# The phase features of the first self-attention: folding, squares and products move from GpSimd and VectorE, and the division by the root mean square comes last

## The chip, the core and the metric

One core of a Trainium2 chip runs the whole program, a transformer of four layers with 14 stages of its own kind. The core has TensorE (PE), VectorE (DVE), ScalarE (ACT), GpSimd (POOL) and SyncE (SP), each with its own queue of instructions; they wait for each other on semaphores. The metric is the time of one execution on the device in microseconds, as the median of several; lower is better.

## What is computed

The change lies in layer 0's self-attention. With 1024 tokens (32 sequences of 32), 256 channels in 16 heads of 16, it builds, besides the usual query and key, a sine and a cosine feature of each, scaled by a normalized amplitude:

```python
def _amp_norm(t):
    a = jax.nn.softplus(t)
    return a / jnp.sqrt(jnp.mean(a * a, axis=-1, keepdims=True) + AMP_EPS)
...
q_amp = _amp_norm(q)
k_amp = _amp_norm(k)
q_phi = math.pi * jnp.tanh(split(x @ Wqp))
k_phi = math.pi * jnp.tanh(split(x @ Wkp))
q_cos = q_amp * jnp.cos(q_phi)
q_sin = q_amp * jnp.sin(q_phi)
k_cos = k_amp * jnp.cos(k_phi)
k_sin = k_amp * jnp.sin(k_phi)
scores_phase = (einsum(q_cos, k_cos) + einsum(q_sin, k_sin)) * scale
lam = (LAMBDA_MAX * jnp.tanh(lambda_raw))[None, :, None, None]
scores = scores_dot + lam * scores_phase
```

## The kernel before

The program is a list of stages. Each stage is one block: every engine gets its own straight list of instructions, the order is the order in which the code is written, and a barrier of all engines ends the stage. `phase_features` is such a stage. `prepare` (projections) runs ahead of it and leaves queries and keys in `qk` and the raw phases in `ph`, both 128 partitions x 2 halves x 2048 numbers: half u=0 is of the queries, u=1 of the keys, channels lie on partitions and tokens along the row. `self_attention` follows, and takes `qk`, `sn` and `cs`.

In the stage, softplus(t) is built as max(t, 0) + ln(1 + exp(-|t|)) with a correction for the rounding of 1 + exp. VectorE makes the magnitudes (line 1625), ScalarE the exp (1668), VectorE "plus" and "rest" (1628, 1631), ScalarE the Ln (1672), VectorE the sum, the amplitude and its square (1635, 1638, 1640). TensorE sums the squares of each head of 16 channels, with tokens on partitions (1709: for each half 16 products with a 0/1 matrix of 8 columns, into PSUM bank 4 or 5). ScalarE takes the root (1682), VectorE the reciprocal (1645), ScalarE spreads each value over its 16 channels (1687), and TensorE transposes the result back, four transposes for a PSUM bank of 512 columns, eight banks in all (1717). VectorE multiplies the amplitude by each bank (1650).

Beside this, ScalarE takes tanh of the phases (1665), then the sine (1676) and, as sin(pi/2 - pi |x|), the cosine (1679). The magnitude |x| for it is made by GpSimd as 2 max(x, 0) - x, in `cs` (1695 and 1697). Last come the products of sine and cosine with the normalized amplitude: those of the queries with half of tanh(lambda) as well, on VectorE (1656, for each of the two rows of 1024), the cosine of the keys on VectorE (1658), the sine of the keys on GpSimd (1700).

The functions `stage`, `buffers` and `spread` are helpers; `k.ps` is PSUM with 8 banks.

Of the kernel before, what the change touches and what calls it, by code (L numbers as in the profile page):

```python
# [18 lines left out]
ALU = mybir.AluOpType  # L19
ACT = mybir.ActivationFunctionType  # L20
# [8 lines left out]
DC = D // P  # L29
# [183 lines left out]
@contextmanager  # L213
def stage(k, names):

    k.stages += 1
    sems = {n: k.nc.alloc_semaphore(name=f"{n}_{k.stages}") for n in names.split()}
    clear_retired(k)
    with k.nc.Block() as block:
        yield block, namedtuple("Semaphores", sems)(**sems)  # L220
    k.retired = list(sems.values())
# [9 lines left out]
@contextmanager  # L231
def buffers(k, dtype=F32, **shapes):

    with ExitStack() as ctx:
        k.buffers += 1
        made = {n: ctx.enter_context(k.nc.sbuf_tensor(f"{n}_{k.buffers}", list(s), dtype)) for n, s in shapes.items()}
        yield namedtuple("Buffers", made)(**made)
# [51 lines left out]
def spread(ap, n, axis):  # L289

    shape = list(ap.shape)
    return ap.unsqueeze(axis).broadcast_to(shape[:axis] + [n] + shape[axis:])
# [1316 lines left out]
def phase_features(k, w, qk, ph, amp, sn, cs):  # L1609


    nc = k.nc
    PI = float(np.float32(np.pi))
    names = ("abs_done exp_done plus_done rest_done ln_done sum_done amp_done square_done sums_done root_done recip_done spread_done wide_done "
             "norm_done tanh_done rise_done fold_done sin_done cos_done lam_tanh lam_done const_done")
    with stage(k, names) as (block, s), \
            buffers(k, f=[P, 2, DC, T], rms=[P, 2, 2, NT, DC, 8], eps=[P, 1], half=[P, 1], lam=[P, 2, DC]) as b:
        def roots(u):

            return b.f[:, u].rearrange("p c t -> p (c t)").rearrange("p (a ch) -> p a ch", ch=P)  # L1620

        @block.vector
        def _(dve):
            for u in range(2):
                nc.vector.scalar_tensor_tensor(amp[:, u], qk[:, u], -1.0, qk[:, u], ALU.mult, ALU.max).then_inc(s.abs_done, 1)
            for u in range(2):
                dve.wait_ge(s.exp_done, u + 1)
                nc.vector.tensor_scalar(b.f[:, u], amp[:, u], 1.0, None, ALU.add).then_inc(s.plus_done, 1)
                dve.wait_ge(s.plus_done, u + 1)

                nc.vector.scalar_tensor_tensor(amp[:, u], b.f[:, u], -1.0, amp[:, u], ALU.add,
                                               ALU.subtract).then_inc(s.rest_done, 1)
            for u in range(2):
                dve.wait_ge(s.ln_done, u + 1)
                nc.vector.scalar_tensor_tensor(b.f[:, u], qk[:, u], 0.0, b.f[:, u], ALU.max, ALU.add).then_inc(s.sum_done, 1)
                dve.wait_ge(s.sum_done, u + 1)
                dve.wait_ge(s.rest_done, u + 1)
                nc.vector.tensor_tensor(amp[:, u], b.f[:, u], amp[:, u], ALU.subtract).then_inc(s.amp_done, 1)
                dve.wait_ge(s.amp_done, u + 1)
                nc.vector.tensor_tensor(b.f[:, u], amp[:, u], amp[:, u], ALU.mult).then_inc(s.square_done, 1)  # L1640
            dve.wait_ge(s.lam_tanh, 1)
            nc.vector.tensor_scalar(b.lam[:, 1], b.lam[:, 0], 0.5, None, ALU.mult).then_inc(s.lam_done, 1)
            for u in range(2):
                dve.wait_ge(s.root_done, u + 1)
                nc.vector.reciprocal(b.rms[:, 1, u], b.rms[:, 0, u]).then_inc(s.recip_done, 1)
            for u in range(2):
                for q in range(4):
                    dve.wait_ge(s.wide_done, 4 * u + q + 1)
                    part = amp[:, u, q // 2, (q % 2) * 512:(q % 2) * 512 + 512]
                    nc.vector.tensor_tensor(part, part, k.ps[:, 4 * u + q, :], ALU.mult).then_inc(s.norm_done, 1)  # L1650
            dve.wait_ge(s.norm_done, 8)
            dve.wait_ge(s.lam_done, 1)
            for done, t in ((s.sin_done, sn), (s.cos_done, cs)):
                dve.wait_ge(done, 2)
                for c in range(DC):
                    nc.vector.scalar_tensor_tensor(t[:, 0, c], t[:, 0, c], b.lam[:, 1, c:c + 1], amp[:, 0, c],
                                                   ALU.mult, ALU.mult)
            nc.vector.tensor_tensor(cs[:, 1], cs[:, 1], amp[:, 1], ALU.mult)

        @block.scalar  # L1660
        def _(act):
            act.wait_ge(*w.at)
            nc.scalar.activation(b.lam[:, 0], w.lam, ACT.Tanh).then_inc(s.lam_tanh, 1)
            for u in range(2):
                nc.scalar.activation(ph[:, u], ph[:, u], ACT.Tanh).then_inc(s.tanh_done, 1)
            for u in range(2):
                act.wait_ge(s.abs_done, u + 1)
                nc.scalar.activation(amp[:, u], amp[:, u], ACT.Exp, scale=-1.0).then_inc(s.exp_done, 1)
            for u in range(2):
                act.wait_ge(s.plus_done, u + 1)  # L1670
                act.wait_ge(s.rest_done, u + 1)
                nc.scalar.activation(b.f[:, u], b.f[:, u], ACT.Ln).then_inc(s.ln_done, 1)
            act.wait_ge(s.tanh_done, 2)
            act.wait_ge(s.const_done, 2)
            for u in range(2):
                nc.scalar.activation(sn[:, u], ph[:, u], ACT.Sin, scale=PI).then_inc(s.sin_done, 1)
            for u in range(2):
                act.wait_ge(s.fold_done, u + 1)
                nc.scalar.activation(cs[:, u], cs[:, u], ACT.Sin, bias=b.half[:, 0:1], scale=-PI).then_inc(s.cos_done, 1)
            for u in range(2):  # L1680
                act.wait_ge(s.sums_done, u + 1)
                nc.scalar.activation(b.rms[:, 0, u].rearrange("p t c h -> p (t c h)"), k.ps[:, 4 + u, 0:P], ACT.Sqrt,
                                     bias=b.eps[:, 0:1], scale=1.0 / 16).then_inc(s.root_done, 1)
            for u in range(2):
                act.wait_ge(s.recip_done, u + 1)
                inverse = b.rms[:, 1, u].rearrange("p t c h -> p (t c h)")
                nc.scalar.copy(roots(u).rearrange("p a (h d) -> p (a h) d", d=16), spread(inverse, 16, 2)).then_inc(s.spread_done, 1)

        @block.gpsimd
        def _(pool):  # L1690
            nc.gpsimd.memset(b.eps[:], 1e-6).then_inc(s.const_done, 1)
            nc.gpsimd.memset(b.half[:], PI / 2).then_inc(s.const_done, 1)
            for u in range(2):
                pool.wait_ge(s.tanh_done, u + 1)
                nc.gpsimd.tensor_scalar(cs[:, u], ph[:, u], 0.0, 2.0, ALU.max, ALU.mult).then_inc(s.rise_done, 1)
                pool.wait_ge(s.rise_done, u + 1)
                nc.gpsimd.tensor_tensor(cs[:, u], cs[:, u], ph[:, u], ALU.subtract).then_inc(s.fold_done, 1)
            pool.wait_ge(s.norm_done, 8)
            pool.wait_ge(s.sin_done, 2)
            nc.gpsimd.tensor_tensor(sn[:, 1], sn[:, 1], amp[:, 1], ALU.mult)  # L1700

        @block.tensor
        def _(pe):
            for u in range(2):
                pe.wait_ge(s.square_done, u + 1)
                for t in range(NT):
                    for c in range(DC):
                        at = (t * DC + c) * 8
                        mm = nc.tensor.matmul(k.ps[:, 4 + u, at:at + 8], b.f[:, u, c, t * P:(t + 1) * P], k.head8,
                                              start=True, stop=True)  # L1710
                mm.then_inc(s.sums_done, 1)
            for u in range(2):
                pe.wait_ge(s.spread_done, u + 1)
                for c in range(DC):
                    for half in range(2):
                        for t in range(4):
                            mm = nc.tensor.transpose(k.ps[:, 4 * u + 2 * c + half, t * P:(t + 1) * P],
                                                     roots(u)[:, (half * 4 + t) * DC + c, :], k.ident)
                        mm.then_inc(s.wide_done, 1)
# [1091 lines left out]
```

## Time and profile before

| | us |
|---|---|
| median of 3 executions | 2239.22 (2233.44 to 2244.39) |
| the profiled execution | 2251.26, its span 2249.4 |
| granted TensorE clock in it, mean share of full speed | 0.829 |
| VectorE busy in the span | 1016.7 (45%) |
| ScalarE busy | 733.2 (33%) |
| GpSimd busy | 484.8 (22%) |
| TensorE matmuls busy | 1676.2 (75%) |

The shares are means over all stages. The stage of this change stands around 269 to 344 us of the span. A timeline row shows when a run of equal instructions starts, how long it lasts in all, and in brackets for how long the engine stood idle before and on whom it waited.

### The profile page before, as it was taken

Reading aid. Unit: us, or ns where it says so; the run is one execution under the profiler, and the core shown is the slowest. Engines: PE = TensorE matmul, PEld = TensorE weight load, DVE = VectorE, ACT = ScalarE, POOL = GpSimd, SP = SyncE. Lnnn points to the kernel's source line nnn. Section 1 sums busy time; section 2 is a strip of 40 time slices with the busy share of each in tenths; the row PEclk is TensorE's granted clock in tenths of the full one; section 3 lists DMA queues with packets and bytes.
Section 4 is the critical chain, followed back from the end, with each engine's and each line's share of the span. In section 5 each row is a group of like instructions: output and inputs, shape, how many; then the busy total and the mean of one; then the engine's idle time right before and its main releaser. Section 6 shows DMA issues by size and latency. Waiting matters only on the chain. (4 is left out here: it accounts for less than half of the span.)

```text
span 2249.4 us, 54254 instructions
## 1 busy us (share of the span) xinstructions
PE 1676.2 (75%) x22206; PEld 1443.7 (64%) x22206; DVE 1016.7 (45%) x2187; ACT 733.2 (33%) x1631; POOL 484.8 (22%) x643
## 2 busy tenths in 40 slices
PE   5998635769966888674888479976488967767684
PEld 4886535569965777563777368863377945655583
DVE  5565483321126777326111446544755733334313
ACT  3554331114433455220233145431223322322121
POOL 3442242002223333100344222210002200010141
PEclk9999755569988999765999689997687988666697
DMA  3220000049962110003899511100100162000485
GB/s 136 55 50 18 3 0 3 27 159 343 342 239 69 45 41 26 5 4 103 265 309 298 175 30 44 47 27 0 40 23 29 38 215 72 4 2 9 144 282 179
DMA packets 84817, 219.27 MB, mean 97 GB/s; under 512 B 19720, under 2 KB 38472, under 8 KB 77072
## 3 DMA queue, kind: packets, MB, share of 16 engines
q1 hardware_dynamic: 76464, 194.14, 26.2%
q0 software_dynamic: 8160, 22.29, 3.1%
q8 instruction: 153, 2.51, 0.5%
q14 instruction: 40, 0.33, 0.0%
HBM read 200.92 MB, written 15.34 MB: 96 GB/s over the span
## 5 line engine op out<-in xcount | busy, mean ns | idle before, releaser
L2227 ACT ACTIVATE g<-ps,b 128x128 f32<-128x128 f32 x340 | 125.0, 368 | 288.7 <-PE ps L2189 267.4
L2189 PEld LDWEIGHTS ps<-xt,w 128*128 128x128 f32 x1728 | 212.6, 197 | 8.7 <-issue 4.2
L2189 PE MATMUL ps<-xt,w 128*128 128x128 f32 x1728 | 213.5, 280 | 2.7 <-DVE xt L2368 2.1
L2199 PE MATMUL ps<-w,g 128*128 128x256 f32 x864 | 206.6, 387 | 0.0
L2199 PEld LDWEIGHTS ps<-w,g 128*128 128x128 f32 x864 | 161.2, 195 | 19.4
L2245 POOL DMA_INDIRECT x<-rows,token x85 | 83.3, 980 | 316.7 <-DVEq L2344 283.0
L484 PE MATMUL ps<-x,w 128*128 128x512 f32 x408 | 119.9, 460 | 34.8 <-DVE x L581 34.8
L2250 POOL DMA_INDIRECT results<-y,dest x85 | 83.7, 985 | 284.2 <-DVE y L2381 225.6
L2368 DVE COPY xt<-ps 128x256 f32<-128x256 f32 x85 | 36.1, 425 | 235.6 <-PE ps L2179 235.6
L484 PEld LDWEIGHTS ps<-x,w 128*128 128x128 f32 x408 | 91.9, 229 | 61.1 <-DVE x L581 39.9
L468 PE MATMUL ps<-consts_sb,z_sb 128*128 128x128 f32 x176 | 34.9, 365 | 112.1 <-DVE z_sb L567 112.0
L468 PEld LDWEIGHTS ps<-consts_sb,z_sb 128*128 128x128 f32 x176 | 28.4, 188 | 119.3 <-DVE z_sb L567 117.8
L733 PE MATMUL ps<-c,w 128*128 128x258 f32 x512 | 97.7, 304 | 8.5 <-DVE pt L1031 4.6
L733 PEld LDWEIGHTS ps<-c,w 128*128 128x128 f32 x512 | 78.3, 198 | 21.9 <-issue 11.5
L743 PE MATMUL ps<-w,c 128*128 128x256 f32 x512 | 91.5, 291 | 0.0
L769 PE MATMUL ps<-consts_sb,p 128*128 128x128 f32 x512 | 68.8, 277 | 28.6 <-ACT key L859 28.5
L2381 DVE TENSOR_TENSOR y<-ps,b 128x256 f32<-128x256 f32 x62 | 26.3, 425 | 132.7 <-PE ps L2199 132.7
L1913 PE MATMUL ps<-x,w 128*128 128x512 f32 x288 | 80.0, 419 | 7.7 <-DVE w L2052 7.7
L869 ACT ACTIVATE p<-sc,nmax 128x257 f32<-128x257 f32 x128 | 58.3, 503 | 82.3 <-DVE nmax L996 82.3
L2179 PE MATMUL ps<-consts_sb,x 128*128 128x128 f32 x170 | 35.9, 295 | 61.8 <-DMA x<-rows,token 61.6
L984 DVE TENSOR_TENSOR val<-ps,store_sb 128x512 f32<-128x512 f32 x64 | 44.2, 691 | 83.3 <-PE ps L743 82.9
L1926 PEld LDWEIGHTS ps<-w,g 128*128 128x128 f32 x576 | 76.3, 194 | 7.8 <-issue 3.6
(410 smaller groups left out, 3744.3 us busy)
## 6 DMA issues: line engine op xcount, KB each, us to landing
w<-in_L_ffn_w SPq DMA_DIRECT2D x124, 512.0 KB, 4.9
w<-in_L_ffn_w SPq DMA_DIRECT2D x46, 1024.0 KB, 7.5
c<-in_ctx SPq DMA_DIRECT2D x96, 258.0 KB, 2.7
b<-in_w_L_ffn SPq DMA_DIRECT2D x62, 128.0 KB, 6.7
rows<-in_w_L_xattn SPq DMA_DIRECT2D x8, 768.0 KB
c<-in_w_L_xattn SPq DMA_DIRECT2D x8, 514.0 KB
back<-results SPq DMA_DIRECT2D x16, 256.0 KB, 4.5
raw<-in_L_ffn_w SPq DMA_DIRECT2D x16, 256.0 KB, 3.5
```

The source lines that it names most:

```text
L468: mm = nc.tensor.transpose(k.ps[:, 2 * half + c, t * P:(t + 1) * P], z[:, half * HT + t, c * P:(c + 1) * P], k.ident)
L484: mm = nc.tensor.matmul(bank, r.w[:, p1, c, col:col + P], r.x[:, p2, c, half * 512:(half + 1) * 512], start=i == 0 and c == 0, stop=i == 2 ...
L733: last = nc.tensor.matmul(k.ps[:, KB + c, 0:LP], wp, cp, start=t == 0, stop=t == 4)
L743: last = nc.tensor.matmul(k.ps[:, VB, half * D:(half + 1) * D], cp, wp, start=t == 0, stop=t == 4)
L769: last = nc.tensor.transpose(k.ps[:, TB + pair, at:at + P], b.p[:, par, r4, half * P:(half + 1) * P], k.ident)
L1913: mm = nc.tensor.matmul(k.ps[:, slot(j, h), :], r.w1[:, j // 2, p1, c, h * P:(h + 1) * P], r.x[:, p2, c, (j % 2) * 512:(j % 2 + 1) * 512], ...
L1926: mm = nc.tensor.matmul(k.ps[:, 4 + t, 0:D], r.g[:, p1, slot(j, h), t * P:(t + 1) * P], r.w2[:, j // 2, p2, h, :], start=h == 0 and i == 0 ...
L2189: mm = nc.tensor.matmul(hidden_bank(par, h), b.w1[:, par, c, h * P:(h + 1) * P], b.xt[:, par, c, :], start=c == 0, stop=c == DC - 1)
L2199: mm = nc.tensor.matmul(k.ps[:, YB + par, 0:D], b.g[:, par, h, :], b.w2[:, par, h, :], start=h == 0, stop=h == HC - 1)
L2227: nc.scalar.activation(b.g[:, par, h, :], hidden_bank(par, h), func, bias=b.b1[:, par, h:h + 1]).then_inc(s.g_ready, 1)
L2245: nc.gpsimd.indirect_dma_start(b.x[:, n % 2, :], None, k.rows, bass.IndirectOffsetOnAxis(ap=u.token[:, n:n + 1], axis=0)).then_inc(x_loade ...
L2250: nc.gpsimd.indirect_dma_start(k.results, bass.IndirectOffsetOnAxis(ap=u.dest[:, n:n + 1], axis=0), b.y[:, n % 2, :], None).then_inc(sent[ ...
```

## The change

GpSimd has no block in the stage any more. Its three kinds of work go elsewhere: the two constants are set by VectorE, |x| is one ScalarE activation (Abs) for each half, and the sine of the keys is multiplied on VectorE. The squares go from VectorE to ScalarE (Square), the first between the sines and the cosines, the second behind the cosines. The second tanh goes behind the exps.

The order of the last products is turned round. Before, the amplitude was divided by its root mean square (eight products with PSUM banks) and then multiplied into sine and cosine. Now sine and cosine are multiplied by the raw amplitude (and lambda) first, and then each of them by the PSUM banks: sixteen products. TensorE waits for both roots before it writes the transposes, as it did before through the order of the work.

```diff
         @block.vector
         def _(dve):
+            nc.vector.memset(b.eps[:], 1e-6).then_inc(s.const_done, 1)
+            nc.vector.memset(b.half[:], PI / 2).then_inc(s.const_done, 1)
...
-                dve.wait_ge(s.amp_done, u + 1)
-                nc.vector.tensor_tensor(b.f[:, u], amp[:, u], amp[:, u], ALU.mult).then_inc(s.square_done, 1)
...
+            dve.wait_ge(s.amp_done, 2)
+            dve.wait_ge(s.lam_done, 1)
+            for done, t in ((s.sin_done, sn), (s.cos_done, cs)):
+                dve.wait_ge(done, 1)
+                for c in range(DC):
+                    nc.vector.scalar_tensor_tensor(t[:, 0, c], t[:, 0, c], b.lam[:, 1, c:c + 1], amp[:, 0, c],
+                                                   ALU.mult, ALU.mult).then_inc(s.scaled, 1)
+                dve.wait_ge(done, 2)
+                nc.vector.tensor_tensor(t[:, 1], t[:, 1], amp[:, 1], ALU.mult).then_inc(s.scaled, 1)
...
+            dve.wait_ge(s.scaled, 6)
             for u in range(2):
                 for q in range(4):
                     dve.wait_ge(s.wide_done, 4 * u + q + 1)
-                    part = amp[:, u, q // 2, (q % 2) * 512:(q % 2) * 512 + 512]
-                    nc.vector.tensor_tensor(part, part, k.ps[:, 4 * u + q, :], ALU.mult).then_inc(s.norm_done, 1)
...
+                    for t in (sn, cs):
+                        part = t[:, u, q // 2, (q % 2) * 512:(q % 2) * 512 + 512]
+                        nc.vector.tensor_tensor(part, part, k.ps[:, 4 * u + q, :], ALU.mult)
...
         @block.scalar
         def _(act):
...
+            nc.scalar.activation(ph[:, 1], ph[:, 1], ACT.Tanh).then_inc(s.tanh_done, 1)
+            for u in range(2):
+                act.wait_ge(s.tanh_done, u + 1)
+                nc.scalar.activation(cs[:, u], ph[:, u], ACT.Abs).then_inc(s.fold_done, 1)
...
+            act.wait_ge(s.amp_done, 1)
+            nc.scalar.activation(b.f[:, 0], amp[:, 0], ACT.Square).then_inc(s.square_done, 1)
...
+            act.wait_ge(s.amp_done, 2)
+            nc.scalar.activation(b.f[:, 1], amp[:, 1], ACT.Square).then_inc(s.square_done, 1)
...
-        @block.gpsimd
-        def _(pool):
...
-                nc.gpsimd.tensor_scalar(cs[:, u], ph[:, u], 0.0, 2.0, ALU.max, ALU.mult).then_inc(s.rise_done, 1)
-                pool.wait_ge(s.rise_done, u + 1)
-                nc.gpsimd.tensor_tensor(cs[:, u], cs[:, u], ph[:, u], ALU.subtract).then_inc(s.fold_done, 1)
-            pool.wait_ge(s.norm_done, 8)
-            pool.wait_ge(s.sin_done, 2)
-            nc.gpsimd.tensor_tensor(sn[:, 1], sn[:, 1], amp[:, 1], ALU.mult)
...
         def _(pe):
...
+            pe.wait_ge(s.root_done, 2)
```

The compiled order of ScalarE's instructions in the stage, the kernel before against the changed one; `ACT_TABLE_LOAD` brings in the tables of the functions that follow:

```order
-L1663 ACT_TABLE_LOAD
-L1663 ACTIVATE lam<-store_sb 128x2
-L1665 ACTIVATE ph<-ph 128x2048 x2
-L1668 ACTIVATE amp<-amp 128x2048 x2
-L1672 ACT_TABLE_LOAD
-L1672 ACTIVATE f<-f 128x2048 x2
-L1676 ACT_TABLE_LOAD
-L1676 ACTIVATE sn<-ph 128x2048 x2
-L1679 ACTIVATE cs<-cs,half 128x2048 x2
-L1682 ACT_TABLE_LOAD
-L1682 ACTIVATE rms<-ps,eps 128x128 x2
-L1687 COPY f<-rms 128x2048 x2
```

```order
+L1671 ACT_TABLE_LOAD
+L1671 ACTIVATE lam<-store_sb 128x2
+L1672 ACTIVATE ph<-ph 128x2048
+L1675 ACTIVATE amp<-amp 128x2048 x2
+L1676 ACTIVATE ph<-ph 128x2048
+L1679 ACTIVATE cs<-ph 128x2048 x2
+L1683 ACT_TABLE_LOAD
+L1683 ACTIVATE f<-f 128x2048 x2
+L1686 ACT_TABLE_LOAD
+L1686 ACTIVATE sn<-ph 128x2048 x2
+L1688 ACTIVATE f<-amp 128x2048
+L1691 ACTIVATE cs<-cs,half 128x2048 x2
```

Four activations of 128x2048 are added (1679 twice, 1688, and 1693 behind the cosines), the second tanh stands behind the exps, and the number of table loads is the same: the fourth one, for the root, stands behind 1693.

VectorE's part from the amplitudes on, of the kernel before and then of the changed one, first half of the banks:

```order
-L1638 TENSOR_TENSOR amp<-f,amp 128x2048
-L1640 TENSOR_TENSOR f<-amp 128x2048
-L1642 TENSOR_SCALAR lam<-lam 128x2
-L1645 RECIPROCAL rms<-rms 128x128 x2
-L1650 TENSOR_TENSOR amp<-amp,ps 128x512 x8
-L1656 SCALAR_TENSOR_TENSOR sn<-sn,lam,amp 128x1024 x2
-L1656 SCALAR_TENSOR_TENSOR cs<-cs,lam,amp 128x1024 x2
-L1658 TENSOR_TENSOR cs<-cs,amp 128x2048
```

```order
+L1636 TENSOR_TENSOR amp<-f,amp 128x2048
+L1653 SCALAR_TENSOR_TENSOR sn<-sn,lam,amp 128x1024 x2
+L1656 TENSOR_TENSOR sn<-sn,amp 128x2048
+L1653 SCALAR_TENSOR_TENSOR cs<-cs,lam,amp 128x1024 x2
+L1656 TENSOR_TENSOR cs<-cs,amp 128x2048
+L1659 RECIPROCAL rms<-rms 128x128 x2
+L1666 TENSOR_TENSOR sn<-sn,ps 128x512
+L1666 TENSOR_TENSOR cs<-cs,ps 128x512
```

The products with sine and cosine have moved from behind the reciprocals and banks to ahead of them, and the bank products are pairs, eight pairs in all.

## Rows read from the trace of the kernel before

**Rows 1.** The page's first line: the span and the instructions

```profile
span 2249.4 us, 54254 instructions
```

**Rows 2.** Busy time by stretch: stretch, length, each engine, granted clock, DMA share, GB/s

```profile
262.00:346.00 84.00, 25.15 (x134) 24.10 (x132) 66.96 (x35) 31.35 (x26) 34.08 (x10) 0.59 0.00 0
```

**Rows 3.** VectorE's timeline of the stage: start us, duration us, instruction, idle before

```profile
275.90 5.64 DVE L1628 TENSOR_SCALAR f<-amp 128x2048 f32<-128x2048 f32 x1 [2.39 <-ACT amp L1668]
281.58 6.46 DVE L1631 SCALAR_TENSOR_TENSOR amp<-f,amp 128x2048 f32<-128x2048 f32 x1
287.96 8.09 DVE L1628 TENSOR_SCALAR f<-amp 128x2048 f32<-128x2048 f32 x1
296.09 6.46 DVE L1631 SCALAR_TENSOR_TENSOR amp<-f,amp 128x2048 f32<-128x2048 f32 x1
302.47 2.28 DVE L1635 SCALAR_TENSOR_TENSOR f<-qk,f 128x2048 f32<-128x2048 f32 x1
...
307.11 2.29 DVE L1640 TENSOR_TENSOR f<-amp 128x2048 f32<-128x2048 f32 x1
...
323.74 0.95 DVE L1645 RECIPROCAL rms<-rms 128x128 f32<-128x128 f32 x1 [5.90 <-ACT rms L1682]
326.70 0.69 DVE L1650 TENSOR_TENSOR amp<-amp,ps 128x512 f32<-128x512 f32 x1 [2.01 <-PE ps L1717]
...
328.41 3.85 DVE L1650 TENSOR_TENSOR amp<-amp,ps 128x512 f32<-128x512 f32 x6 [0.17 <-PE ps L1717]
332.30 6.81 DVE L1656 SCALAR_TENSOR_TENSOR sn<-sn,lam,amp 128x1024 f32<-128x1024 f32 x2
339.04 2.47 DVE L1656 SCALAR_TENSOR_TENSOR cs<-cs,lam,amp 128x1024 f32<-128x1024 f32 x2
341.43 2.28 DVE L1658 TENSOR_TENSOR cs<-cs,amp 128x2048 f32<-128x2048 f32 x1
```

**Rows 4.** ScalarE's timeline of the stage

```profile
268.97 1.28 ACT L1663 ACT_TABLE_LOAD   x1 [1.82 <-PEq L219]
...
270.38 3.69 ACT L1665 ACTIVATE ph<-ph 128x2048 f32<-128x2048 f32 x2
...
302.64 1.91 ACT L1672 ACTIVATE f<-f 128x2048 f32<-128x2048 f32 x1 [11.32 <-DVE amp L1631]
...
305.86 3.71 ACT L1676 ACTIVATE sn<-ph 128x2048 f32<-128x2048 f32 x2
309.48 3.88 ACT L1679 ACTIVATE cs<-cs,half 128x2048 f32<-128x2048 f32 x2
```

**Rows 5.** GpSimd's timeline of the stage

```profile
272.36 8.10 POOL L1695 TENSOR_SCALAR cs<-ph 128x2048 f32<-128x2048 f32 x1 [2.98 <-ACT ph L1665]
280.55 5.34 POOL L1697 TENSOR_TENSOR cs<-cs,ph 128x2048 f32<-128x2048 f32 x1
285.86 9.11 POOL L1695 TENSOR_SCALAR cs<-ph 128x2048 f32<-128x2048 f32 x1
295.06 5.34 POOL L1697 TENSOR_TENSOR cs<-cs,ph 128x2048 f32<-128x2048 f32 x1
332.34 4.49 POOL L1700 TENSOR_TENSOR sn<-sn,amp 128x2048 f32<-128x2048 f32 x1 [31.94 <-DVE amp L1650]
```

**Rows 6.** Groups of instructions by form, VectorE: busy us, mean ns, idle before

```profile
L554 DVE MEMSET eps<- 128x1 f32 x14 | 0.8, 59 | 4.7 <-PEq L219 4.7
```

**Rows 7.** TensorE's timeline of the stage

```profile
309.46 13.85 PE L1709 MATMUL ps<-consts_sb,f 128*128 128x8 f32 x64 [41.50 <-DVE f L1640]
325.55 5.34 PE L1717 MATMUL ps<-consts_sb,f 128*128 128x128 f32 x32 [2.24 <-ACT f L1687]
```

**Rows 8.** Busy time by stretch of 50 us, columns as in rows 2

```profile
350.00:400.00 50.00, 35.93 (x1428) 30.32 (x1427) 12.90 (x29) 9.80 (x20) 9.12 (x10) 0.53 0.02 4
...
500.00:550.00 50.00, 50.00 (x346) 47.11 (x346) 5.94 (x14) 20.02 (x55) 13.08 (x14) 1.00 0.95 337
```

More of the change, by code:

```diff
@@ L1614, in phase_features @@
     names = ("abs_done exp_done plus_done rest_done ln_done sum_done amp_done square_done sums_done root_done recip_done spread_done wide_done "
-             "norm_done tanh_done rise_done fold_done sin_done cos_done lam_tanh lam_done const_done")
+             "tanh_done fold_done sin_done cos_done lam_tanh lam_done const_done scaled")
     with stage(k, names) as (block, s), \
@@ L1623, in _, with plus @@
         def _(dve):
-            for u in range(2):
-                nc.vector.scalar_tensor_tensor(amp[:, u], qk[:, u], -1.0, qk[:, u], ALU.mult, ALU.max).then_inc(s.abs_done, 1)
-            for u in range(2):
+            def plus(u):
                 dve.wait_ge(s.exp_done, u + 1)
@@ L1632, in _, with amplitude @@
                                                ALU.subtract).then_inc(s.rest_done, 1)
-            for u in range(2):
+            def amplitude(u):
                 dve.wait_ge(s.ln_done, u + 1)
@@ L1638, in _ @@
                 nc.vector.tensor_tensor(amp[:, u], b.f[:, u], amp[:, u], ALU.subtract).then_inc(s.amp_done, 1)
-                dve.wait_ge(s.amp_done, u + 1)
-                nc.vector.tensor_tensor(b.f[:, u], amp[:, u], amp[:, u], ALU.mult).then_inc(s.square_done, 1)
+            nc.vector.memset(b.eps[:], 1e-6).then_inc(s.const_done, 1)
+            nc.vector.memset(b.half[:], PI / 2).then_inc(s.const_done, 1)
+            for u in range(2):
+                nc.vector.scalar_tensor_tensor(amp[:, u], qk[:, u], -1.0, qk[:, u], ALU.mult, ALU.max).then_inc(s.abs_done, 1)
+            for u in range(2):
+                plus(u)
             dve.wait_ge(s.lam_tanh, 1)
@@ L1643, in _ @@
             for u in range(2):
+                amplitude(u)
+            dve.wait_ge(s.amp_done, 2)
[7 more added lines that the diff above has]
+                nc.vector.tensor_tensor(t[:, 1], t[:, 1], amp[:, 1], ALU.mult).then_inc(s.scaled, 1)
+            for u in range(2):
                 dve.wait_ge(s.root_done, u + 1)
                 nc.vector.reciprocal(b.rms[:, 1, u], b.rms[:, 0, u]).then_inc(s.recip_done, 1)
+            dve.wait_ge(s.scaled, 6)
             for u in range(2):
@@ L1648, in _ @@
                     dve.wait_ge(s.wide_done, 4 * u + q + 1)
-                    part = amp[:, u, q // 2, (q % 2) * 512:(q % 2) * 512 + 512]
-                    nc.vector.tensor_tensor(part, part, k.ps[:, 4 * u + q, :], ALU.mult).then_inc(s.norm_done, 1)
[L1651 to L1658, printed above, removed]
+                    for t in (sn, cs):
+                        part = t[:, u, q // 2, (q % 2) * 512:(q % 2) * 512 + 512]
+                        nc.vector.tensor_tensor(part, part, k.ps[:, 4 * u + q, :], ALU.mult)
         @block.scalar
@@ L1663, in _ @@
             nc.scalar.activation(b.lam[:, 0], w.lam, ACT.Tanh).then_inc(s.lam_tanh, 1)
-            for u in range(2):
-                nc.scalar.activation(ph[:, u], ph[:, u], ACT.Tanh).then_inc(s.tanh_done, 1)
+            nc.scalar.activation(ph[:, 0], ph[:, 0], ACT.Tanh).then_inc(s.tanh_done, 1)
             for u in range(2):
@@ L1668, in _ @@
                 nc.scalar.activation(amp[:, u], amp[:, u], ACT.Exp, scale=-1.0).then_inc(s.exp_done, 1)
+            nc.scalar.activation(ph[:, 1], ph[:, 1], ACT.Tanh).then_inc(s.tanh_done, 1)
+            for u in range(2):
+                act.wait_ge(s.tanh_done, u + 1)
+                nc.scalar.activation(cs[:, u], ph[:, u], ACT.Abs).then_inc(s.fold_done, 1)
             for u in range(2):
@@ L1672, in _ @@
                 nc.scalar.activation(b.f[:, u], b.f[:, u], ACT.Ln).then_inc(s.ln_done, 1)
-            act.wait_ge(s.tanh_done, 2)
             act.wait_ge(s.const_done, 2)
@@ L1687, in _ @@
                 nc.scalar.copy(roots(u).rearrange("p a (h d) -> p (a h) d", d=16), spread(inverse, 16, 2)).then_inc(s.spread_done, 1)
-        @block.gpsimd
-        def _(pool):
[L1691 to L1694, printed above, removed]
-                nc.gpsimd.tensor_scalar(cs[:, u], ph[:, u], 0.0, 2.0, ALU.max, ALU.mult).then_inc(s.rise_done, 1)
-                pool.wait_ge(s.rise_done, u + 1)
-                nc.gpsimd.tensor_tensor(cs[:, u], cs[:, u], ph[:, u], ALU.subtract).then_inc(s.fold_done, 1)
-            pool.wait_ge(s.norm_done, 8)
-            pool.wait_ge(s.sin_done, 2)
-            nc.gpsimd.tensor_tensor(sn[:, 1], sn[:, 1], amp[:, 1], ALU.mult)
         @block.tensor
```

## The prediction

> **What bounds the kernel now.** The program is a chain of stages with a barrier between each two, so I asked where in the span of 2249.4 us [rows 1] the changed stage stands and what ends last in it. The view of busy time by stretch, cut at the stage's edges (262 to 346 us), shows that no engine is at its limit there: VectorE (DVE) is busy 67 of 84 us, TensorE 25, ScalarE (ACT) 31, GpSimd (POOL) 34, and the DMA engines move nothing [rows 2]. The stage is a chain of dependent steps, and no transfer runs under it that could become the limit once it is shorter. It starts with a table load on ACT at 268.97 and ends with VectorE's last product at 341.43 + 2.28 = 343.71, so it is 74.7 us long [rows 3, 4].
>
> Read VectorE's timeline first [rows 3]. Lines 1635 and 1640 take 2.28 and 2.29 us for 128x2048 with two SBUF inputs. Line 1631 is the same kind and shape as line 1635, yet it takes 6.46. Line 1628 takes 5.64 and then 8.09. Line 1656 is four equal instructions: the sn pair takes 6.81 us, the cs pair 2.47. Now lay GpSimd's timeline beside it [rows 5]. GpSimd's instructions end at 280.46, 285.89, 294.97 and 300.40. VectorE's end at 281.54, 288.04, 296.05 and 302.55: 1.08, 2.15, 1.08 and 2.15 us later. At the stage's end GpSimd finishes its product at 336.83, while the first sn instruction of line 1656 is still open. Each of these VectorE instructions is long as if it stood still until GpSimd's was done, and then ran in its own time. I read this as: while GpSimd works in SBUF, these VectorE instructions do not move. So 275.90 to 302.55, 26.65 us, is GpSimd's time on VectorE's account, and ACT stands waiting for it (11.32 us ahead of the second Ln alone [rows 4]).
>
> The Trainium skill says so too ("Advanced Engine Details and Errata", the notes on VectorE's two SBUF ports): the second one is shared with GpSimd, and the instructions of the one block those of the other. Its "VectorE: DVE Perf Modes" (the perf-mode tier table) gives 1227 ns for a lone fp32 tensor_scalar of 2048; with the trace's 1.08 or with this figure the sum below is the same.
>
> **The change, step by step**, on the clock of the trace. I rebuild the stage with durations of rows, and put its end against 343.71.
>
> ACT becomes the first bound. From 270.38 it runs six 128x2048 instructions in a row (tanh, exp, exp, tanh, abs, abs). Pairs of such take 3.69 us, 1.845 each [rows 4]: 11.1 us, to 281.5. What they wait for is there: VectorE's first magnitude is done at about 269.1 + 2.3 = 271.4 and the second at 273.6 (the two memsets that it now runs first are 0.06 each [rows 6]); the first exp can start at 272.2. Abs is nowhere in the trace. Every other function of this shape takes 3.69 to 3.88 a pair [rows 4], so its bounds are 1.84 and 1.94 each; I take 1.845, and two of them and two Squares can be 0.4 us off. The compiled order shows four table loads in the stage before and after.
>
> VectorE under it: plus and rest for each half. The first exp ends at 274.1. Line 1628 alone is at least the remainder of 1.08 and at most the 2.29 of a two-input product; rest is 2.28. So both halves are done between 280.9 and 283.3, and the second is needed at 284.7. Either end is hidden behind ACT. That is where VectorE's stall goes.
>
> ACT goes on: table load 1.28 (as in [rows 4]) to 282.8; Ln and Ln, the first ends at 284.7, the second at 286.5; table load to 287.8; two Sin, 3.71, to 291.5; Square of half 0, 1.85, to 293.35; two cosines, 3.88, to 297.2; Square of half 1, to 299.1. VectorE's amplitudes come at 284.7 + 2 x 2.28 = 289.3 and 293.9, both before their Squares. So half 0's Square is late by the sine ahead of it, about 2 us.
>
> TensorE: the sums of squares are 64 matmuls of line 1709 in 13.85 us [rows 7], 6.93 a half and back to back. They now run from 293.4 to 300.3 and on to 307.25; the second Square is done long before 300.3. Before, they ended at 323.31. This is the gain of the first part: **16.1 us**.
>
> From the last sum to VectorE's first product with a PSUM bank the way is the same: root, reciprocal, spread copy on ACT, four transposes. It was 326.70 - 323.31 = 3.39 us [rows 3, 7]. The new wait (TensorE for both roots) is met before the spread copy, and holds only the transposes. In the shadow of the sums, VectorE now does the scaling by lambda and amplitude: sn 2.47 + 2.28, cs the same, from 293.9 to 303.4. The first half's reciprocal (0.95 us [rows 3]) lands at 304.4, with room to 307.6, where ACT's spread copy first asks for it; were the scaling longer than that, the excess would go straight to the end. So the first bank product starts at 307.25 + 3.4 = 310.65.
>
> The tail: before, 8 bank products to 332.3, then 11.4 us to 343.71 (with GpSimd's product in it, 4.49 us that held VectorE's). Now 16 bank products. Six at full pace took 3.85 us [rows 3], 0.63 from start to start and 0.69 for the last: 15 x 0.632 + 0.69 = 10.2 us. Transposes come at 0.86 us a bank ((328.41 - 326.70) / 2), and each bank now feeds 1.26 us of VectorE, so TensorE isn't late. The end is at 310.65 + 10.2 = **320.8**. Before, it was 17.0 us from the first bank product to the end; now 10.2: **6.8 us**.
>
> Sum: 16.1 + 6.8 = 22.9 us. The following stage waits for the barrier only, nothing is loaded under this one for it, and GpSimd, with no work here now, waits at the barrier as it waits today; so it starts 22.9 us earlier.
>
> One rule of the Trainium skill speaks against the edit ("ScalarE: Activation LUTs", rules for kernel authors): additions and products belong on VectorE. The trace has 1.85 us on ACT against 2.29 on VectorE for 128x2048 fp32. By the rule the Squares would stay on VectorE, right behind each amplitude, and the sums would start at 291.6 and not at 293.4; the stage would then be 1.8 us shorter still, so the rule costs this change a little and does not turn it.
>
> **Rivals.**
> *A: the long VectorE instructions are long by themselves* (in-place, or that operation), not held by GpSimd. For it: both of line 1631 take exactly 6.46. Against it: line 1656, the same pair at 6.81 and at 2.47 within 9 us, and the ends that follow GpSimd's. Worked out: 26.65 us from 274.1 end at 300.8; the second Ln at 302.7; table load and sines to 307.7; Squares at 309.6 and 315.3; sums to 323.5; 3.4 and 10.2 more: 337.0. The gain is 6.7 us, 2232.5.
>
> *B: TensorE's clock helps.* The attention that follows runs at a mean granted 0.53 of full speed (350 to 400 us), close to the 1.2 GHz level [rows 8]. It would start 8 us after the last transpose, not 15.9 before. If more of it is granted 2.4 GHz, some of its 36 us of matmuls in each 50 are shorter: 10 us more, about 2206. Other phases of those lifts, without a trend, are worth 3 us to either side.
>
> *C: slower.* The expert loop that follows is at 50.00 of 50 us of TensorE at a granted 1.00, in three such stretches from 500 to 650 [rows 8]. If the shifted start makes the clock stay at 1.2 GHz there, 150 us of full-speed work is worth up to 150 us more. It decides from the point where 23 us of it fall to the lower level; for 2250 it takes 34. Nothing shows the clock to fall under such a load, and the loop's own entry is not changed. 3 in 100.
>
> *D: the change doesn't do what it says*: GpSimd's seven instructions of the stage are gone in the compiled order, so that is excluded; what is left is Abs and Square at twice the price on ACT; three of them (both Abs and the first Square), 5.6 us, are on the path: 2221.9. 3 in 100, inside the range.
>
> **The numbers.** The profiled execution was 2251.26 us, 12 above the median of 2239.22; the difference of two stage lengths carries over unchanged: 2239.2 - 22.9 = 2216.3. Forecast 80 in 100 (with D), A 8, B 8, C 3, something unseen 1. The forecast's own range is 3 us of clock phase, 2 of durations, and the 5 us by which single executions stand off the median: 2208 to 2225. For 8 in 10 I take in part of A and all of B: 2206 to 2229. A measurement of this kernel can tell 0.5%, 11.2 us, from no change, so "faster" is below 2228: the forecast and B give 0.88. Same, 0.09, is A and a forecast that misses by half; slower 0.03.
>
> **What would show it.** VectorE's lines for plus and rest at about 1.1 and 2.3 us (if 6, A holds). ACT without a wait until the second Square. First sum at 24.4 us after the stage's first table load, first bank product at 41.7, end at 51.8. Sixteen bank products 0.63 apart. If the stage is 52 us long and the total hasn't fallen by 23, look at the granted clock between 320 and 500 us.

## The result, and the profile after

The changed kernel took 2212.51 us (median of 4; 2207.03 to 2220.06), beside 2240.95 us for the kernel before in the same measurement: ratio 0.988, 95% interval 0.9841 to 0.9919. Two further series of it gave 0.9899 (0.9867 to 0.9931) and 0.989 (0.9861 to 0.9918). The change makes the kernel faster, by some 25 us: 0.989 of 2240 is 24.6 us off. The profiled execution has a span of 2218.2 us.

The stage itself went from 74.74 us to 51.20 (from its first table load to the end of VectorE's last product, 268.39 to 319.59), 23.5 us less. First ScalarE's timeline in the changed kernel: start us, duration us, instruction, and in brackets the idle time before it with its cause. It answers to [rows 4].

```profile
268.39 1.28 ACT L1671 ACT_TABLE_LOAD   x1 [1.82 <-PEq L219]
...
277.00 3.69 ACT L1679 ACTIVATE cs<-ph 128x2048 f32<-128x2048 f32 x2
280.71 1.28 ACT L1683 ACT_TABLE_LOAD   x1
282.00 3.71 ACT L1683 ACTIVATE f<-f 128x2048 f32<-128x2048 f32 x2
...
287.03 3.71 ACT L1686 ACTIVATE sn<-ph 128x2048 f32<-128x2048 f32 x2
290.64 1.89 ACT L1688 ACTIVATE f<-amp 128x2048 f32<-128x2048 f32 x1
...
306.45 0.37 ACT L1696 ACTIVATE rms<-ps,eps 128x128 f32<-128x128 f32 x1 [6.46 <-PE ps L1710]
```

From 269.69 to 298.14 no row has a wait; the 11.32 us of [rows 4] are gone. Abs (line 1679) takes 3.69 us a pair, as every other function does, and Square (1688) 1.89 alone.

VectorE's timeline, against [rows 3]; lines 1626 and 1628 are the plus and rest that were 1628 and 1631:

```profile
273.52 1.23 DVE L1626 TENSOR_SCALAR f<-amp 128x2048 f32<-128x2048 f32 x1 [0.53 <-ACT amp L1675]
274.79 2.29 DVE L1628 SCALAR_TENSOR_TENSOR amp<-f,amp 128x2048 f32<-128x2048 f32 x1
276.99 1.22 DVE L1626 TENSOR_SCALAR f<-amp 128x2048 f32<-128x2048 f32 x1
278.25 2.29 DVE L1628 SCALAR_TENSOR_TENSOR amp<-f,amp 128x2048 f32<-128x2048 f32 x1
...
302.32 0.94 DVE L1659 RECIPROCAL rms<-rms 128x128 f32<-128x128 f32 x1
306.84 0.95 DVE L1659 RECIPROCAL rms<-rms 128x128 f32<-128x128 f32 x1 [3.58 <-ACT rms L1696]
309.94 0.69 DVE L1666 TENSOR_TENSOR sn<-sn,ps 128x512 f32<-128x512 f32 x1 [2.14 <-PE ps L1719]
310.54 0.68 DVE L1666 TENSOR_TENSOR cs<-cs,ps 128x512 f32<-128x512 f32 x1
...
318.91 0.68 DVE L1666 TENSOR_TENSOR cs<-cs,ps 128x512 f32<-128x512 f32 x1
```

The same four instructions that took 5.64, 6.46, 8.09 and 6.46 us with GpSimd at work beside them take 1.23, 2.29, 1.22 and 2.29. The scaling and the first reciprocal are over at 303.26, well before the second root, and VectorE then waits 3.58 us for it. The sixteen bank products run without a gap, 0.60 us from start to start. TensorE's timeline, against [rows 7]:

```profile
292.59 13.82 PE L1710 MATMUL ps<-consts_sb,f 128*128 128x8 f32 x64 [25.20 <-ACT f L1688]
308.74 5.80 PE L1719 MATMUL ps<-consts_sb,f 128*128 128x128 f32 x32 [2.33 <-ACT f L1701]
```

| from the stage's first table load, us | before | forecast | after |
|---|---|---|---|
| start of the first sum of squares | 40.5 | 24.4 | 24.2 |
| end of the last sum of squares | 54.3 | 38.3 | 38.0 |
| start of the first bank product | 57.7 | 41.7 | 41.6 |
| end of the stage | 74.7 | 51.8 | 51.2 |

### The profile page after: what moved, and what is told of

The parts are those of the page before. It is cut to its first block and busy times, and to the rows that moved or that the text cites. A ratio compares the mean times of both kernels' runs of the same rounds, so it can differ in the third digit from the quotient of the medians.

```text
span 2218.2 us, 54260 instructions
## 1 busy us (share of the span) xinstructions
PE 1674.4 (75%) x22206; PEld 1440.5 (65%) x22206; DVE 993.9 (45%) x2196; ACT 737.2 (33%) x1635; POOL 452.2 (20%) x636
## 5 line engine op out<-in xcount | busy, mean ns | idle before, releaser
L2201 PE MATMUL ps<-w,g 128*128 128x256 f32 x864 | 202.8, 382 | 0.0
L1928 PE MATMUL ps<-w,g 128*128 128x256 f32 x576 | 77.7, 286 | 3.5 <-DVE g L2028 3.5
```

The costliest lines, as they stand in the source:

```text
L1928: mm = nc.tensor.matmul(k.ps[:, 4 + t, 0:D], r.g[:, p1, slot(j, h), t * P:(t + 1) * P], r.w2[:, j // 2, p2, h, :], start=h == 0 and i == 0 ...
L2201: mm = nc.tensor.matmul(k.ps[:, YB + par, 0:D], b.g[:, par, h, :], b.w2[:, par, h, :], start=h == 0, stop=h == HC - 1)
```

## The experiments

The theory: 18 us of the gain are VectorE's freedom from GpSimd's folding; the rest is the turned order of the products and GpSimd's last product. The rival: the long VectorE instructions were long by the old order or by themselves. All stage lengths below are measured as above. Most of them repeat closely: 51.20 us in all three traces of the changed kernel, 45.31 and 45.32 in two of the reordered one, and 74.74 and 74.56 in two of the kernel before. One kernel, the first below, has 57.65 and 56.62. The totals do not repeat so well, which has its own paragraph below.

**One part alone: Abs on ScalarE in the kernel before.**

```diff
+            for u in range(2):
+                act.wait_ge(s.tanh_done, u + 1)
+                nc.scalar.activation(cs[:, u], ph[:, u], ACT.Abs).then_inc(s.fold_done, 1)
...
-                nc.gpsimd.tensor_scalar(cs[:, u], ph[:, u], 0.0, 2.0, ALU.max, ALU.mult).then_inc(s.rise_done, 1)
-                pool.wait_ge(s.rise_done, u + 1)
-                nc.gpsimd.tensor_tensor(cs[:, u], cs[:, u], ph[:, u], ALU.subtract).then_inc(s.fold_done, 1)
```

> The kernel before with one part of the change alone: |x| for the cosine is ScalarE's Abs, GpSimd does no folding. Squares, the order of the products and GpSimd's last product stay. If GpSimd's folding held VectorE, plus and rest take 1.2 and 2.3 us and not 5.6 to 8.1, the sums of squares end about 36.2 us after the stage's first table load (before 54.3), and the stage is 56.6 us long (before 74.7): 18 us less, about 2222. If plus and rest are long by themselves, they stay at 26.6 us together and the stage loses at most 5 us.

Plus and rest took 1.23, 2.29, 1.22 and 2.29 us, the sums of squares ended 36.4 us into the stage, and the stage was 57.65 us long, 17.1 less than before. Its tail still had GpSimd's last product. VectorE's timeline of this kernel near the stage's end, and under it GpSimd's:

```profile
319.31 6.82 DVE L1656 SCALAR_TENSOR_TENSOR sn<-sn,lam,amp 128x1024 f32<-128x1024 f32 x2
326.05 2.47 DVE L1656 SCALAR_TENSOR_TENSOR cs<-cs,lam,amp 128x1024 f32<-128x1024 f32 x2
...
319.35 4.49 POOL L1698 TENSOR_TENSOR sn<-sn,amp 128x2048 f32<-128x2048 f32 x1 [45.87 <-DVE amp L1650]
```

Two equal pairs of VectorE, 6.82 beside GpSimd and 2.47 without: 4.35 us of waiting for a product that costs VectorE 2.28 if it does it itself. The total however was only 10.5 us lower (ratio 0.9951, 0.9933 to 0.9968), which left 6 us unexplained, so it ran again:

> The kernel before with ScalarE's Abs for the folding, again. Its stage was 17.1 us shorter, but its total only 10.5 (7 to 15). If the missing 6 us are scatter of the other stages, this run gives 17 within 4 us. If GpSimd's absence costs something later, it gives 10 again.

It gave 0.9922 (0.9896 to 0.9948), 17.5 us, with a stage of 56.62 us. Here the stage's gain is carried over in full. The first interval alone did not contain 17, and why that total gained less is not shown; the paragraph on scatter comes back to it. The two stages differ by 1.03 us at the transposes: TensorE took 6.67 us for them at a granted clock of 0.54 in the first trace, and 5.03 us at 0.73 in the second. In the first, VectorE waited for a transpose before six more of its eight banks, which then start 0.85 us apart; in the second before two, and the others start 0.60 apart.

**The folding given back to GpSimd, in the changed kernel.**

```diff
-                nc.scalar.activation(cs[:, u], ph[:, u], ACT.Abs).then_inc(s.fold_done, 1)
...
+                nc.gpsimd.tensor_scalar(cs[:, u], ph[:, u], 0.0, 2.0, ALU.max, ALU.mult).then_inc(s.rise_done, 1)
+                pool.wait_ge(s.rise_done, u + 1)
+                nc.gpsimd.tensor_tensor(cs[:, u], cs[:, u], ph[:, u], ALU.subtract).then_inc(s.fold_done, 1)
```

> The changed kernel with the folding given back to GpSimd, all else as changed. Holding by GpSimd: VectorE's plus and rest go back to 5 to 8 us each, ending 1.1 and 2.2 us behind GpSimd's instructions; the stage is about 69.8 us long against the changed kernel's 51.2, so 18.6 us slower than it, about 2231. If the stall came from something else in the old order (the second tanh ahead of the exps), the stage stays near 51 to 55.

The stage was 69.52 us long; 69.8 had been expected. The total was 2231.13 (ratio 0.9984, 0.997 to 0.9997). VectorE's timeline rows of this kernel, then GpSimd's:

```profile
273.90 7.50 DVE L1626 TENSOR_SCALAR f<-amp 128x2048 f32<-128x2048 f32 x1 [0.53 <-ACT amp L1675]
281.44 6.46 DVE L1628 SCALAR_TENSOR_TENSOR amp<-f,amp 128x2048 f32<-128x2048 f32 x1
287.82 8.09 DVE L1626 TENSOR_SCALAR f<-amp 128x2048 f32<-128x2048 f32 x1
295.95 6.46 DVE L1628 SCALAR_TENSOR_TENSOR amp<-f,amp 128x2048 f32<-128x2048 f32 x1
...
272.16 8.16 POOL L1705 TENSOR_SCALAR cs<-ph 128x2048 f32<-128x2048 f32 x1 [40.87 <-ACT ph L1672]
280.41 5.34 POOL L1707 TENSOR_TENSOR cs<-cs,ph 128x2048 f32<-128x2048 f32 x1
285.73 9.11 POOL L1705 TENSOR_SCALAR cs<-ph 128x2048 f32<-128x2048 f32 x1
294.92 5.34 POOL L1707 TENSOR_TENSOR cs<-cs,ph 128x2048 f32<-128x2048 f32 x1
```

The first plus starts 1.8 us sooner behind GpSimd's start than in the kernel before (273.90 - 272.16 against 275.90 - 272.36), and takes 7.50 where it took 5.64: it ends 1.08 us behind GpSimd's instruction in both (281.40 - 280.32; 281.54 - 280.46). The length of this VectorE instruction is set by when GpSimd ends. With the old order gone and the folding back, the stall is back. The rival falls.

**The folding on GpSimd in small pieces**, for how the hold works.

```diff
+                for c in range(DC):
+                    for j in range(4):
+                        part, x = (a[:, u, c, j * 256:(j + 1) * 256] for a in (cs, ph))
+                        nc.gpsimd.tensor_scalar(part, x, 0.0, 2.0, ALU.max, ALU.mult).then_inc(s.rise_done, 1)
+                        pieces += 1
+                        pool.wait_ge(s.rise_done, pieces)
+                        last = nc.gpsimd.tensor_tensor(part, part, x, ALU.subtract)
```

> The changed kernel with the folding on GpSimd in 16 pieces of 256 columns, for how the hold works. If a VectorE instruction stands still until GpSimd's current instruction ends, it now waits for at most one piece (0.9 us): plus takes at most 2.1 us and rest 3.2, and all four are over about 17 us into the stage. If the two engines share bandwidth, plus and rest stay at 5 to 8 us each. GpSimd's folding ends late (about 37 us into the stage) and delays the second cosine and Square, so the stage is about 62 us long either way.

VectorE's timeline of this kernel, and under it GpSimd's, three instructions early and two late:

```profile
274.57 1.23 DVE L1626 TENSOR_SCALAR f<-amp 128x2048 f32<-128x2048 f32 x1 [0.53 <-ACT amp L1675]
275.83 2.29 DVE L1628 SCALAR_TENSOR_TENSOR amp<-f,amp 128x2048 f32<-128x2048 f32 x1
278.04 1.75 DVE L1626 TENSOR_SCALAR f<-amp 128x2048 f32<-128x2048 f32 x1
279.82 2.36 DVE L1628 SCALAR_TENSOR_TENSOR amp<-f,amp 128x2048 f32<-128x2048 f32 x1
...
272.83 3.21 POOL L1709 TENSOR_SCALAR cs<-ph 128x256 f32<-128x256 f32 x1 [40.83 <-ACT ph L1672]
276.13 2.58 POOL L1712 TENSOR_TENSOR cs<-cs,ph 128x256 f32<-128x256 f32 x1
278.68 2.04 POOL L1709 TENSOR_SCALAR cs<-ph 128x256 f32<-128x256 f32 x1
...
301.79 1.07 POOL L1709 TENSOR_SCALAR cs<-ph 128x256 f32<-128x256 f32 x1
302.94 0.72 POOL L1712 TENSOR_TENSOR cs<-cs,ph 128x256 f32<-128x256 f32 x1
```

The first four rows are VectorE's: held by 0.5 us at most, and all over 12.7 us into the stage (282.18 - 269.44). With whole instructions they had been held by 4.2 to 6.9 us each. A steady sharing of bandwidth would slow them as much beside pieces as beside whole instructions, so it is out: VectorE waits at most about as long as a piece. Only part of this fits a wait for the other's whole instruction. The second plus ends 1.08 us behind GpSimd's (279.79 and 278.71), as before. But the rest at 279.82 took 2.36 us, 0.07 more than alone, although GpSimd's instruction was open until 280.72, and the first plus at 274.57 was not held at all although GpSimd's had been open since 272.83. GpSimd's spans in a profile are rough, and what decides who goes first, and at what grain, these runs do not show. The hold works both ways, which I had not said: GpSimd's pieces take 3.21 and 2.58 us beside VectorE's instructions, and 1.07 and 0.72 alone. Cutting the pieces turned the wait over to GpSimd. Its folding ended 50 us into the stage and not at 37, since each piece has a cost of its own (16 x (1.07 + 0.72) = 28.6 us without any hold, against 22.7 for the four whole instructions with 6.94 and 4.4 of their own, estimated from [rows 5] less VectorE's share) and was held by VectorE besides. The stage was 74.3 us long where I had said 62. There is a single execution of this kernel, of 2236.21 us, from which nothing follows for the total.

**The other part alone: the turned order of the products in the kernel before**, with GpSimd folding.

```diff
+            dve.wait_ge(s.scaled, 6)
...
-                    part = amp[:, u, q // 2, (q % 2) * 512:(q % 2) * 512 + 512]
-                    nc.vector.tensor_tensor(part, part, k.ps[:, 4 * u + q, :], ALU.mult).then_inc(s.norm_done, 1)
+                    for t in (sn, cs):
+                        part = t[:, u, q // 2, (q % 2) * 512:(q % 2) * 512 + 512]
+                        nc.vector.tensor_tensor(part, part, k.ps[:, 4 * u + q, :], ALU.mult)
...
-            nc.gpsimd.tensor_tensor(sn[:, 1], sn[:, 1], amp[:, 1], ALU.mult)
```

> The kernel before with the other part alone: sine and cosine are multiplied by lambda and the raw amplitude first, by the PSUM banks last (16 products), the keys' sine on VectorE; GpSimd folds and VectorE squares as before. The sums of squares still end at 54.3 us of the stage. VectorE's scaling (9.5 us) starts at 47.2 and ends at 56.7, after the sums, so the reciprocals and the first bank product come 3 us later than before; then 10.2 us: stage 71 us against 74.7, about 4 us less, 2236. If the parts simply added, it would be 6.8 us less.

The stage was 70.54 us long, 4.2 less than before, and the total 0.9988 (0.9969 to 1.0008), which a total can't tell from no change. The parts do not quite add: 17.1 (18.1 in the second trace of the other part) and 4.2 make 21.3 to 22.3, and both together gave 23.5. Alone, the turned order has the end of its scaling (9.5 us in all) in the open, since VectorE's last square ends only 7 us before the sums (315.98 and 323.04 in that trace); the spread copies waited 2.91 us for the reciprocals behind it. It needs the squares off VectorE to be hidden.

**The squares back on VectorE**, the rest as changed:

```diff
+                dve.wait_ge(s.amp_done, u + 1)
+                nc.vector.tensor_tensor(b.f[:, u], amp[:, u], amp[:, u], ALU.mult).then_inc(s.square_done, 1)
...
-            nc.scalar.activation(b.f[:, 0], amp[:, 0], ACT.Square).then_inc(s.square_done, 1)
...
-            nc.scalar.activation(b.f[:, 1], amp[:, 1], ACT.Square).then_inc(s.square_done, 1)
```

> The changed kernel with the squares back on VectorE, each right behind its amplitude. The prediction said 1.8 us shorter, since the sums start at once. Worked out again with VectorE's own queue: two squares (4.6 us) push the scaling to 38.5 us of the stage, and the reciprocals stand behind it, so the first bank product comes at 42.6 and not 41.5: the sums end 1.7 us earlier, the stage is 1 us longer, 52.2 us. The trace decides it by the stage's length; the total can't.

Who waited for whom in this kernel's stage: us in total, times, longest.

```profile
ACT rms L1694 <- PE ps L1708: 8.6, 2, 6.5
...
ACT f L1699 <- DVE rms L1661: 2.6, 1, 2.6
```

The sums ended 36.4 us into the stage, 1.6 earlier than in the changed kernel, and then ScalarE's spread copy (line 1699) waited 2.6 us for the reciprocals, which stand in VectorE's queue behind the scaling. The stage was 52.32 us, 1.1 longer. Total 0.991 (0.988 to 0.994).

**A stage filled up to its old length**:

```diff
+            for i in range(10):
+                if i:
+                    dve.wait_ge(s.filled, i)
+                nc.vector.tensor_tensor(b.f[:, 0], amp[:, 0], amp[:, 1], ALU.mult).then_inc(s.filled, 1)
```

> The changed kernel with ten extra products of 128x2048 on VectorE at the end of the stage (23 us, their result is used nowhere), so that the next stage starts as late after this one's start as in the kernel before. If the change saves only the stage's own time, this costs 23 us and stands 5 us below the kernel before, at about 2235. If the 3 us that attention lost with the change hang on how long TensorE has been idle ahead of it (8 us now, 15.9 before, 31 here), attention is back at 100 us and the total at 2240.

The stage was 74.34 us and the total 2240.5, ratio 0.9996 (0.9975 to 1.0017) to the kernel before. With the stage's gain taken back, the total's gain is gone too, and if anything else remains of the change it is within that interval, some 4 to 6 us to either side. The attention behind it took 98.1 us after 31 us of idle TensorE, within the 96.3 to 100.4 that the kernel before shows in its two traces with 15.9 us. In the two traces of the reordered version below, with 8.6 us of idle time in both, the attentions lie 3.9 us apart. No dependence on the idle time ahead of it shows above that scatter.

**How much totals scatter.** The kernel before was measured against itself, and the changed kernel twice more:

> The kernel before itself, run as if it were a changed one, beside the kernel before: what is left of a difference here is what such a comparison can't tell. Expected 1.000, within 3 us.

> The changed kernel again, to narrow its interval. The stage alone gives 23.5 us; if the total gain is really 28, some 5 us lie in later stages.

> The changed kernel once more. Its stage is 23.5 us shorter than before's; if the stage's gain carries over in full, the total is 23.5 us lower, within the few us by which other stages scatter.

The kernel before against itself gave 1.0009 (0.9993 to 1.0024). Yet its profiled execution here has a span of 2227.4 us, and the one of [rows 1] 2249.4: 22 us between two executions of one program, as much as the change is worth. Here are three of its stretches, bounds chosen at the same stages (the first one begins 0.18 us earlier in the upper view), in the trace of [rows 1] and then in the new one (stretch, length, busy us of each engine, granted clock, DMA share, GB/s): the attention behind the changed stage, the last attention, and the second expert stage.

```profile
343.71:444.29 100.58, 72.15 (x2768) 60.18 (x2768) 25.05 (x56) 20.38 (x41) 14.93 (x17) 0.55 0.02 4
2004.42:2065.71 61.29, 47.08 (x1616) 37.73 (x1616) 19.90 (x40) 20.38 (x41) 4.69 (x2) 0.64 0.02 4
1029.90:1277.10 247.20, 176.89 (x1112) 162.39 (x1112) 65.46 (x159) 59.05 (x159) 76.67 (x78) 0.86 0.75 245
```

```profile
341.59:437.90 96.31, 68.43 (x2768) 57.54 (x2768) 25.05 (x56) 20.36 (x41) 14.92 (x17) 0.60 0.02 4
1989.12:2045.98 56.86, 44.15 (x1616) 35.91 (x1616) 19.89 (x40) 20.36 (x41) 4.69 (x2) 0.67 0.02 4
1023.95:1267.31 243.36, 177.47 (x1112) 162.63 (x1112) 65.37 (x159) 58.95 (x159) 76.64 (x78) 0.86 0.76 249
```

Same instructions, same counts. With the bounds made equal, the attentions are 4.1 and 4.4 us shorter where the granted clock was 0.60 and 0.67, not 0.55 and 0.64; the expert stage is 3.8 us shorter at the same clock and 249 GB/s, not 245. Why the levels fall as they do in a given execution is not shown by any run here. It means that the spans of two single executions can't say what this change does to the total. The length of the changed stage says what it does there, and the series of totals have to confirm it. They do so only to some us: in the series with Abs alone, the folding given back, the turned order alone and the squares on VectorE, all four ratios were taken against one median of the kernel before (2233.97), and all four gains, 10.9, 3.6, 2.7 and 20.1 us by the ratios, stand below those of their stages (17.1, 5.2, 4.2 and 22.4). Why is not shown.

**A version that beats both.** From the changed kernel's trace: the first Square stands behind a sine though its amplitude is there at 288.56, the two Abs stand ahead of the Ln, and the spread copy of the first half, whose reciprocal is done at 303.26, stands behind the second root until 306.71.

```diff
+            fold(0)
             for u in range(2):
...
                 nc.scalar.activation(b.f[:, u], b.f[:, u], ACT.Ln).then_inc(s.ln_done, 1)
...
                 nc.scalar.activation(sn[:, u], ph[:, u], ACT.Sin, scale=PI).then_inc(s.sin_done, 1)
+                if u == 0:
+                    square(0)
+            fold(1)
+            square(1)
...
-            for u in range(2):
                 act.wait_ge(s.recip_done, u + 1)
...
-            pe.wait_ge(s.root_done, 2)
```

On VectorE the first reciprocal goes ahead of the last cosine product. The spread copy of each half stands right behind its root.

> A version meant to beat both: the changed kernel with the first Square ahead of the second sine, the second Abs moved behind the sines, the first half's root, reciprocal and spread copy ahead of the second half's root, and TensorE's transposes of the first half without a wait for the second root. By the durations of the changed kernel's trace the sums start 20.5 us into the stage (24.2 now) and end at 34.3, the first bank product stands at 35.7 (41.5 now), the stage is 45.4 us long (51.2): 5.8 us less, 2207 if the changed kernel is at 2212.5.

> The reordered version once more: stage 29.4 us shorter than before's and 5.9 shorter than the changed kernel's. Expected 5.9 us below the changed kernel in the same runs.

The first series gave 2210.97 us, ratio 0.9874 (0.9843 to 0.9904), the second 2208.93, ratio 0.986 (0.9837 to 0.9883). The stage was 45.31 us long. It beats the kernel before clearly. Against the changed kernel it is 5.4 and 2.3 us lower in the medians of the same series; 5.9 by the stage, which totals with this scatter do not confirm on their own. TensorE's and VectorE's rows:

```profile
287.29 13.82 PE L1725 MATMUL ps<-consts_sb,f 128*128 128x8 f32 x64 [21.61 <-ACT f L1693]
301.07 5.45 PE L1733 MATMUL ps<-consts_sb,f 128*128 128x128 f32 x32
...
301.54 0.95 DVE L1658 RECIPROCAL rms<-rms 128x128 f32<-128x128 f32 x1 [0.31 <-ACT rms L1712]
302.41 0.63 DVE L1676 TENSOR_TENSOR sn<-sn,ps 128x512 f32<-128x512 f32 x1
```

The transposes now follow the sums without a gap (2.33 us in the changed kernel), and what bounds the first bank product is VectorE's own reciprocal of the second half, in front of it.

## Why the prediction was right

- **The stall.** The prediction read 26.65 us of VectorE's time (275.90 to 302.55) as GpSimd's, from instructions of equal shape with unequal lengths and from ends 1.08 and 2.15 us behind GpSimd's. Giving the folding back alone brought the stall back, and moved one instruction's length from 5.64 to 7.50 while its end stayed 1.08 us behind. Rival A, 2232.5 us by its sum, is out. The 26.65 us were put too high: the same four instructions take 7.03 us alone (1.23, 2.29, 1.22 and 2.29), so the hold was 19.6. The sum did not use the 26.65, since it rebuilt the stage from ScalarE's rows. The Trainium skill's sentence ("Advanced Engine Details and Errata", the note that GpSimd and VectorE's two-port instructions block each other) agrees with the traces in the main; the two-input instructions of line 1628, 6.46 us beside GpSimd and 2.29 alone, are held as well. How finely the one holds the other, the trace with the pieces leaves open.
- **ScalarE as the new bound.** Forecast 24.4 us to the first sum, measured 24.2. Abs and Square cost 1.85 and 1.89, inside the bounds that the other functions set, so rival D's doubled price did not come. Plus took 1.23 us, the figure of the Trainium skill ("VectorE: DVE Perf Modes", the perf-mode tier table) and not my 1.08; it lay where either was hidden.
- **The tail.** Sixteen bank products at 0.632 were 10.2 us in the forecast; they took 9.65 (309.94 to 319.59), 0.60 apart. The rate came from a row of [rows 3] that starts behind a wait of 0.17 us for a transpose. In the second trace of the kernel before the same six products took 3.68 us and not 3.85, which is 0.60 from start to start, so the row behind the forecast very likely held 0.17 us of waiting. This is the one mis-sized term that counts, 0.5 us of the 0.6 by which the stage's sum of 22.9 fell short of 23.5.
- **The Square rule.** The prediction said that squares left on VectorE would make the stage 1.8 us shorter. They made it 1.1 longer. The step that failed is that it followed the square to TensorE and not VectorE's own queue: two squares push back the scaling, and the reciprocals behind it. This was a side remark and no term of the sum. The rule of the Trainium skill ("ScalarE: Activation LUTs", rules for kernel authors: products on VectorE), followed in this order of the queue, costs 1.1 us; the advantage that it names is for bf16, and here, in fp32, the product takes 2.29 us on VectorE and 1.89 on ScalarE.
- **The clock (rival B and C).** The attention took 97.3, 96.5 and 97.0 us in three traces of the changed kernel, and 100.4 and 96.3 in two of the one before. The 10 us of B are not there, and the loss of C isn't either: the expert loop ran at a granted 1.00 from 474 to 624 us. The first expert stage took 221.5, 220.8 and 221.6 us in the changed kernel against 218.3 and 218.7 before. It is no effect of the earlier start: with the filled stage it starts as late as before and has 221.1, and in the reordered version, where it starts earliest, it has 219.1 and 219.0. What these 3 us are stays open.
- **The total.** Forecast 2216.3; the three medians were 2212.51, 2216.34 and 2211.2. The first series' 28 us of gain are 23.5 of the stage and some 5 that no stage accounts for; the two further series gained 22.6 and 24.6 by their ratios, so I take the 5 for scatter. That the forecast total lies within 0.1 us of the second median is luck.

## What to carry to other kernels

When instructions of one kind and shape have two lengths in a timeline, lay GpSimd's rows beside VectorE's: ends that follow GpSimd's by a constant point to a hold, and the price of a GpSimd instruction is then up to its own length on VectorE's queue too. Work that looked free on an idle GpSimd was cheaper here on ScalarE (3.69 us for the two Abs, against 19.6 us of hold) and even on VectorE itself (2.28 us for the last product, against 4.35). And before a step is moved to an engine, follow that engine's queue to the next thing that someone waits for.

## What the runs showed of the hardware that I had not expected

- The hold is mutual, and its length follows the length of GpSimd's instructions: with GpSimd in pieces of 256 columns, each VectorE instruction of plus and rest lost 0.5 us at most, and GpSimd's pieces went from 1.07 and 0.72 us to as much as 3.21 and 2.58.
- A ScalarE table load cost 1.3 us from the end of one function to the start of the next (Abs ends at 280.69, Ln starts at 282.00), with nothing else around it.
- Back-to-back VectorE products with a PSUM operand of 512 columns start every 0.60 us, though each is 0.68 long.
- TensorE's 32 transposes took 6.67 us at a granted clock of 0.54 and 5.03 at 0.73, in two traces of one kernel, and its stage was 1.03 us longer for it.
- Two executions of the kernel before differed by 22 us in their spans, spread over many stages.
